# Layer 1 of a graph network: scatter sums over 64 nodes instead of 128, two 64-column matmuls of 193 columns instead of one of 385

## What is computed

```
w   = silu(edge_scalars @ Wfc1/4) @ (Wfc2/8)             # 192 weights per edge
e0, e1 = f0[src], f1[src]                                # 64 scalars, 32 vectors of the source node
mid0 = w0 * e0 * y0            (64)                      # y: 4 numbers per edge
mid1 = w3 * dot(e1, y1) / sqrt(3)   (32)
mid2 = w1 * e0 * y1            (3 x 64)
mid3 = w2 * e1 * y0            (3 x 32)
n    = segment_sum([mid0, mid1, mid2, mid3], dst) / max(count(dst), 1)
out  = x + sc + (n_scalars @ Wa) * (n @ Wl2)             # per node
```

## Time and profile before

| | |
|---|---|
| time, median of 3 runs | 8661.65 us (8655.53 to 8667.87) |
| span of the profiled execution | 8679.9 us |
| PE busy in the span | 7627.6 us (88%) |
| DVE busy | 7274.4 us (84%) |
| POOL busy | 6016.9 us (69%) |
| ACT busy | 3252.4 us (37%) |
| layer 1, first to last gather issue | 6421 to 8600 us of the span |
| last stage (`node2`) | from 8614.9 us |

### The profile page before, as it was taken

How to read it: one execution, slowest core, us unless ns; L and a number is a source line. 1 busy time by engine, 2 the same in 40 slices (tenths; PEclk the granted TensorE clock), 3 DMA queues, 4 the chain that set the end, 5 groups by cost and what they waited for, 6 DMA issues and landing times. The chain is left out here.

```text
span 8679.9 us, 218293 instructions
## 1 busy us (share of the span) xinstructions
PE 7627.6 (88%) x60373; PEld 5771.5 (66%) x60374; DVE 7274.4 (84%) x17597; ACT 3252.4 (37%) x8375; POOL 6016.9 (69%) x5890
## 2 busy tenths in 40 slices
PE   2599999999999999999999999887968888888888
PEld 1487777877877787877787778776644444444445
DVE  4699999999999999999999999775368888888886
ACT  1244444444444444444444444332222222222223
POOL 0477777777777777777777777651037777777774
PEclk9799999999999999999999999987569999999999
DMA  4344444444444444444444444321012222222222
GB/s 53 78 101 99 102 100 101 102 100 101 101 102 101 101 101 99 102 100 100 100 101 102 101 102 100 77 75 29 11 37 67 67 67 67 67 67 67 67 67 61
DMA packets 616622, 725.52 MB, mean 84 GB/s; under 512 B 284132, under 2 KB 390884, under 8 KB 616573
## 3 DMA queue, kind: packets, MB, share of 16 engines
q0 software_dynamic: 225408, 385.00, 20.4%
q1 hardware_dynamic: 391165, 339.92, 15.3%
HBM read 708.40 MB, written 16.06 MB: 83 GB/s over the span
## 5 line engine op out<-in xcount | busy, mean ns | idle before, releaser
L778 PE MATMUL bank_pair<-w_msg,blocks 128*128 128x160 f32 (+2 forms) x15640 | 2078.7, 288 | 126.8 <-DVE blocks L1030 98.2
L720 POOL DMA_INDIRECT got_src<-src_tab,idx x1564 | 1661.5, 1062 | 659.4 <-POOL idx L714 358.5
L778 PEld LDWEIGHTS bank_pair<-w_msg,blocks 128*128 128x128 f32 x15640 | 1972.7, 192 | 218.5 <-DVE blocks L1030 218.5
L1504 POOL DMA_INDIRECT gotf<-f_tab,idx x1568 | 1702.3, 1086 | 514.2 <-issue 477.4
L720 POOL DMA_INDIRECT got_dst<-dst_tab,idx x1564 | 1486.3, 950 | 528.7 <-issue 503.7
L802 PEld LDWEIGHTS bank_pair<-weights_t,product 128*128 128x128 f32 x12896 | 1498.7, 195 | 309.9 <-issue 295.6
L802 PE MATMUL bank_pair<-weights_t,product 128*128 128x128 f32 x12896 | 1575.5, 281 | 9.5 <-ACT weights_t L932 8.2
L1545 PE MATMUL bank_pair<-val,to_node 128*128 128x385 f32 x3136 | 1247.6, 545 | 5.0 <-DVE val L1659 5.0
L1600 ACT ACTIVATE val<-pre,y_edge 128x160 f32<-128x160 f32 x1568 | 542.8, 417 | 1534.0 <-DVE pre L1640 1531.4
L1545 PEld LDWEIGHTS bank_pair<-val,to_node 128*128 128x128 f32 x3136 | 621.6, 208 | 536.8 <-issue 270.1
L767 PE MATMUL bank_pair<-edge,w_edge 64*128 64x512 f32 x3128 | 884.8, 642 | 9.5 <-DVE blocks L1030 9.5
(11 more groups left out here) (268 smaller groups left out, 11950.3 us busy)
## 6 DMA issues: line engine op xcount, KB each, us to landing
rbf<-in_rbf SPq DMA_DIRECT2D x391, 256.0 KB
dst_bc<-in_dst_rows SPq DMA_DIRECT2D x391, 256.0 KB
y<-in_y SPq DMA_DIRECT2D x391, 128.0 KB
y<-in_y SPq DMA_DIRECT2D x391, 96.0 KB
gotf<-f_tab,idx POOLq DMA_INDIRECT x1568, 2.7
got_src<-src_tab,idx POOLq DMA_INDIRECT x1564
got_dst<-dst_tab,idx POOLq DMA_INDIRECT x1564
rbf<-in_rbf SPq DMA_DIRECT2D x392, 32.0 KB, 1.7
```

Of the source, the lines that this page charges most:

```text
L720: pool.indirect_dma_start(out=buf[slot][:, t, :], out_offset=None, in_=table[:, :], in_offset=bass.IndirectOffsetOnAxis(ap=idx[slot][:, c: ...
L778: return nc.tensor.matmul(to, blocks[rows, k, P * t:P * t + P], w_msg[rows, c0:c1], start=start, stop=stop)
L1504: pool.indirect_dma_start(out=got[k][:, t, :], out_offset=None, in_=f_tab[:, :], in_offset=bass.IndirectOffsetOnAxis(ap=idx[k][:, t:t + 1] ...
```

## The change

A pair now sums over a window of 64 nodes (`WIN`), and `marks` counts blocks of 64. The mask has 64 columns for each tile in place of 128. The 385 columns become two halves of 192, each with a column of ones after it (193): half 0 holds the 160 columns that ACT writes and the 32 of L1659, half 1 the 192 of L1652. For each tile two matmuls, with the same mask as stationary operand, write half 0 to PSUM partitions 0 to 63 and half 1 to partitions 64 to 127, on the two 64-column halves of the array. `win` and `total` are then 128 partitions by 193 columns: partition p and p + 64 hold the two halves of the same node. `total` has 99 blocks of 193 columns in place of 50 of 385. In the last stage a tile of 128 nodes takes two blocks: four transposes of 128 columns, and for each half of the nodes four matmuls with a 64-column stationary operand. A small copy on DVE brings the counts to the right partitions, and the set-up has three more small DVE instructions.

```diff
-SUM1 = SUM + 1
+HALF = SUM // 2
+HALF1 = HALF + 1
+WIN = 64
+NB1 = NODES_PAD // WIN
...
-    w_last = sb("w_last", [P, 3, QW - 1])
+    w_last = sb("w_last", [P, 4, QW - 1])
...
-    total = sb("total", [P, NT + 1, SUM1])
+    total = sb("total", [P, NB1 + 1, HALF1])
...
-                    pool.memset(total[:, 0:12, :], 0.0)
+                    pool.memset(total[:, 0:24, :], 0.0)
...
+                    chain.step(dve.tensor_copy(col_i[:], iota_col[:]))
+                    chain.step(dve.tensor_scalar(col_i[:], col_i[:], WIN - 1, None, ALU.bitwise_and))
+                    chain.step(dve.tensor_copy(col[:], col_i[:]))
...
-                    chain.step(dve.tensor_scalar(slot0[:], slot0[:], float(P), None, ALU.is_lt))
+                    chain.step(dve.tensor_scalar(slot0[:], slot0[:], float(WIN), None, ALU.is_lt))
...
-                    chain.step(dve.tensor_scalar(span_i[:], span_i[:], 7, None, ALU.logical_shift_right))
+                    chain.step(dve.tensor_scalar(span_i[:], span_i[:], 6, None, ALU.logical_shift_right))
...
-        to_node = [tmp(f"to_node1{i}", [P, TILES, P]) for i in range(2)]
+        to_node = [tmp(f"to_node1{i}", [P, TILES, WIN]) for i in range(2)]
...
-        win = [psum[3][:, 512 * i:512 * i + SUM1] for i in range(2)]
+        win = [psum[3][:, 512 * i:512 * i + HALF1] for i in range(2)]
...
+                def add_tile(half, nodes, k, t, start, stop):
+                    for side in range(2):
+                        last = nc.tensor.matmul(win[half][WIN * side:WIN * side + WIN, :], nodes,
+                                                val[k][:, t, HALF1 * side:HALF1 * side + HALF1], start=start, stop=stop)
+                    return last
+
...
-                        last = nc.tensor.matmul(win[k // 2], to_node[k % 2][:, t, :], val[k][:, t, :],
-                                                start=k % 2 == 0 and t == 0, stop=k % 2 == 1 and t == TILES - 1)
+                        last = add_tile(k // 2, to_node[k % 2][:, t, :], k, t, k % 2 == 0 and t == 0, k % 2 == 1 and t == TILES - 1)
...
-                    for j, n in enumerate(rows_of):
-                        last = nc.tensor.transpose(pT[t % 2][0:n, j, :], total[:, t, P * j:P * j + n], ident[:])
+                    for j in range(4):
+                        first = WIN * (j % 2)
+                        last = nc.tensor.transpose(pT[t % 2][:, j, :], total[:, 2 * t + j // 2, first:first + P], ident[:])
...
-                    for j, n in enumerate(rows_of):
-                        last = nc.tensor.matmul(pQ[t % 2], turned[t % 2][0:n, j, :], w_last[0:n, j, :], start=j == 0, stop=j == 2)
+                    for k in range(4):
+                        cols = slice(WIN * (k // 2), WIN * (k // 2) + WIN)
+                        for part in range(2):
+                            last = nc.tensor.matmul(pQ[t % 2][WIN * part:WIN * part + WIN, :], turned[t % 2][:, 2 * part + k % 2, cols],
+                                                    w_last[:, k, :], start=k == 0, stop=k == 3)
...
-                    nc.scalar.activation(turned[t % 2][:], pT[t % 2][:, 0:3, :], ACT.Copy).then_inc(S["turned_copied"], 1)
+                    nc.scalar.activation(turned[t % 2][:], pT[t % 2], ACT.Copy).then_inc(S["turned_copied"], 1)
...
+                    for part in range(2):
+                        rows = slice(WIN * part, WIN * part + WIN)
+                        last = dve.tensor_copy(den[rows, :], total[rows, 2 * c * CH + part:2 * (c + 1) * CH:2, HALF])
+                    chain.step(last)
```

More of the change, by code:

```diff
@@ L233, in _ @@
                 for k, frm, c in last_pieces(A):
-                    put(w_last[k % P:k % P + frm.shape[0], k // P, c:c + frm.shape[1]], frm)
+                    half, place = k // HALF, k % HALF
+                    upper = place >= P
+                    place -= WIN if upper else 0
+                    put(w_last[place:place + frm.shape[0], 2 * half + upper, c:c + frm.shape[1]], frm)
                 sp.wait_ge(s_ext, 2)
@@ L479, in last_pieces @@
         for part in range(2):
-            out.append((D + CS * x + 32 * part, v[32 * part:32 * part + 32, :], c))
-    k = D + 3 * CS
+            out.append((HALF + CS * x + 32 * part, v[32 * part:32 * part + 32, :], c))
+    k = D
     out += [(k, s[64:96, :], 0), (k, a[64:96, :], CS)]
@@ L1354, in tmp @@
             return sx.enter_context(nc.sbuf_tensor(name, shape, dt))
-        val = [tmp(f"val{i}", [P, TILES, SUM1]) for i in range(4)]
+        val = [tmp(f"val{i}", [P, TILES, 2 * HALF1]) for i in range(4)]
         slot0 = tmp("slot0", [P, NG_PAD * TILES])
@@ L1362, in layer1 @@
         more_from = tmp("more_from", [1, PAIRS + 1], I32)
-        steps = tmp("steps", [P, 64])
+        steps = tmp("steps", [P, 128])
+        col = tmp("col1", [P, 1])
         with ExitStack() as tx:
@@ L1555, in body @@
                             for t in range(2 * TILES):
-                                last = nc.tensor.matmul(win[half], to_more[:, t, :], val[2 * half + t // TILES][:, t % TILES, :],
-                                                        start=t == 0, stop=t == 2 * TILES - 1)
+                                last = add_tile(half, to_more[:, t, :], 2 * half + t // TILES, t % TILES, t == 0, t == 2 * TILES - 1)
                             last.then_inc(s["more_sum"], 1)
@@ L1670, in merge @@
                     q, half = i * 2 + k // 2, k // 2
-                    row, count = nc.s_assert_within(mark & 63, 0, NT - 1), mark >> 6
+                    row, count = nc.s_assert_within(mark & 127, 0, NB1 - 1), mark >> 7
                     dve.wait_ge(s["window_sum"], q * 2 + 2)
@@ L1684, in more @@
                     done = w * 8
[L1685 removed]
+                    nth = nc.s_assert_within(w - first + 1, 0, 127)
                     def settled(instruction, n):
@@ L1728, in node2 @@
             "turned", "turned_copied", "mapped", "mapped_copied", "ch", "res", "out0", "out1")}
-        turned = [tmp(f"turned{i}", [P, 3, P]) for i in range(2)]
+        turned = [tmp(f"turned{i}", [P, 4, P]) for i in range(2)]
         q = [tmp(f"q{i}", [P, CH, QW - 1]) for i in range(2)]
```

64 lines of the change are left out of this document (33 added, 31 removed).

## The result

The changed kernel takes 8714.6 us, median of 4 runs (8710.43 to 8716.64), against 8660.49 us (4 runs, 8655.53 to 8667.87) for the kernel before, measured beside it: 1.0063 times, 95% interval 1.0049 to 1.0077. It is slower by 54 us, where 73 were forecast. The profiled execution has a span of 8708.6 us, 28.7 more than the one of before. That difference is smaller than the medians' because the profiled execution of before was slow for its kernel: layer 0, which the edit doesn't touch, took 20.3 us more in it than in the one after. From the start of layer 1's set-up (the fill of `total`) to the end, the two executions took 2300.1 and 2349.2 us, 49.1 apart.

The account below looks back on a forecast made before the run. Layer 1's loop was taken as bound by a ring of DVE and gathers, the last stage by PE. Set-up 1, loop 0, further windows 30 and last stage 42 gave +73 us: 8735 us, range 8695 to 8795.

Parts of the forecast that it names:

- The ring: Layer 1's loop: L1636 to end of L1652 3.06 us, held gather's end 0.81, landing 1.72; together 5.59 us.
- one gather of 1.5 us per group: Sign listed for the loop: each group would show a gather of 1.5 us.
- The loop: Layer 1's loop: DVE's 1.16 us saved per pair turns into waiting for rows; 0 taken, bounds -20 and +12 us.
- The window sum on PE: Layer 1's loop: eight slots of two side-by-side passes take 1.7 us against 2.6 before, worth 0.
- The further windows: Layer 1's loop: five pairs spanning 64 nodes or more run `more`; the last four cost +30 us, bounds 21 and 52.
- M: Price of one `more` on DVE in layer 1's loop: 10.9 us, bounds 8.7 and 16.5.
- pair 181 is hidden: Layer 1's loop: this pair's `more` costs nothing, POOL running about 11 us ahead and DVE regaining its lag later.
- The last stage: PE's 49 tiles behind the loop: 2.01 us each, +0.86 per tile, +42 us in all; bounds +19 and +78.
- slots without overhead: Rival: paired passes cost one duration, slots 0.134 and 0.161 us; last stage +19 to 24, M 10.1; 8711 us, chance 0.12.
- the two changes of width: Last stage: PE changing between 128 and 64 columns loses 0.05 us each time, 0.1 per tile.
- The adds: DVE in layer 1's loop: an add of 193 columns takes 0.31 us, 0.31 less each, two per pair.
- the set-up: Ahead of layer 1's loop: three more chained DVE instructions and a few POOL fills, +1.3 us, all on the path.

Follow-up runs that it names:

- e6b_before_late: Kernel before with DVE's product L1652 moved later, behind L1657, same work, run again in the third batch: 8656.20 us, 1.0020 of the kernel before.
- a0_after_again: The changed kernel itself, unaltered, measured once more in the third batch: 8689.57 us, 1.0050 of the kernel before.
- e1_no_more: Changed kernel with the number of further windows set to 0 for all pairs, their edges left out: 8665.82 us, 1.0022 of the kernel before.

## Why the prediction came out as it did

**The direction and the bound were right.** The loop's pace is that of the gathers, and PE and DVE got 38 us per 500 us of relief that turned into waiting. The ring's signs are there as listed: period 5.54 us, DVE waiting for rows in 325 of 343 groups, starts of the two halves together. One sign was too simple: not one gather of 1.5 us per group, but in 206 of 342 groups two held ones, mostly for 0.15 to 0.4 us. And the ring is less than a fixed path: what set the pace in every run is four gathers and their pauses, and the landing and L1652 only decide where the gathers start; `e6b_before_late` missed by taking it for more.

**The loop: 0 taken, -6.9 us up to group 365.** It lies inside the bounds of -20 and +12. The gathers are 5 ns shorter in the mean, and 4 x 0.005 x 365 is 7 us. `a0_after_again` has 2014.4 us for groups 0 to 363, where the two executions of before and after have 2019.0 and 2012.1, so a part of it is the spread between executions. In the first batch three kernels with this same loop took 1997.4 to 1998.2 us for it, so the batch moves it by more than the 6.9.

**The window sum on PE.** 1.53 us at full clock for 16 passes, against 1.7 forecast and 2.86 (eight passes of twice the width) before, and worth nothing in the loop. The granted clock fell from 0.94 to 0.75 with PE busy for 376 instead of 414 us of 500, and that cost nothing either: at the low level the sum takes 2.84 us, and DVE waits 11.2 us for it in all.

PE in the loop of the kernel after, at the full level and, a group later, at the low one; `L1536` and `L1537`, on the two halves of the array, start together.

```profile
7111.40 0.42 PE L1536 MATMUL bank_pair<-rbf,w_fc 16*64 16x256 f32 x1
7111.41 0.42 PE L1537 MATMUL bank_pair<-rbf,w_fc 16*64 16x256 f32 x1
...
7111.98 1.53 PE L1553 MATMUL bank_pair<-val,to_node 128*64 128x193 f32 x16
...
7117.77 2.84 PE L1553 MATMUL bank_pair<-val,to_node 128*64 128x193 f32 x16
```

**The further windows: +30 taken, +29.7 for the last four.** The number of loops, their places and the price held: M comes out at some 10.4 us (the three intervals with a `more` between groups 385 and 391 have a mean of 15.45 us, less the 5.0 of a group with a merge), where 10.9 was put. Inside it terms were off against each other, and that part is luck: the entry takes 0.9 to 1.2 us for 1.5, the eight small steps 1.8 to 2.2 for 2.6, and DVE waits 5.1 to 5.8 us for PE's part, where 4.7 and 0.25 for handing over were put. Wrong was "pair 181 is hidden": it isn't hidden but pays back more than it costs, 10.2 against 17.3 us, because for fourteen groups behind it the gathers are held less. The prediction counted only that DVE regains its lag up to the ring's pace, not that it gets past it.

**The last stage: +42 taken, +33 measured.** This is the term that was mis-sized, and it explains 9 of the 24 us between the sums. The slot was taken from the 16-row pair at 0.184 us where 128 rows give 0.138 (the rival "slots without overhead" had this right), 0.37 us too much in a tile; the two changes of width were put at 0.1 where they cost 0.30, 0.2 too little. Together 1.84 for 2.01 us, by 49.

**The adds** cost 0.42 us for 193 columns where the line through two sizes gave 0.31, but they start 0.33 us apart, and it is hidden in the loop.

Of the 24 us between 73 and 49, 9 are the last stage, 7 the loop up to group 365, 7 pair 181's pay-back and 1 the set-up. The measured 8714.6 lies nearer to the 8711 of the rival "slots without overhead" than to 8735. That is in part luck: the rival was right on the slots, but it put the changes of width at 0 to 0.05 us each, where they cost 0.15, and had neither of the 7 us.

## What to carry to other kernels

When two engines have slack and the loop doesn't get faster, look at what the third one's instructions collide with: here the order of DVE's instructions, with no work added or taken away, was worth 0.5% before the change and over 1% after it, more than the whole change cost. Price a change that narrows tiles at its edges as well: the passes overlap for free, each change of width costs 0.15 us here, where PE is the bound. And a rare branch was free in the middle of a loop with buffers ahead, and four at its end, with nothing behind them to catch up in, cost 33 us of their 42.

## What the runs showed of the hardware

- A gather that starts while a DVE instruction with both inputs in SBUF runs (L1627, L1644 and L1652 before, L1644, L1661 and L1669 after) ends 0.81 to 0.83 us after that instruction does, or after its own 0.945 us if that is later: it can take up to 1.75 us (`e6b_before_late`). The first 0.03 us of the DVE instruction are an exception: in the kernel before, 6500 to 8400 us, 68 gathers start up to 0.034 us behind it and none is held; all 546 that start later than that, with 0.2 us or more of the instruction left, are. The Trainium skill ("SBUF — State Buffer", Who interferes with whom) has a DVE instruction with two SBUF inputs contend with a GpSimd instruction that reads SBUF; the traces agree for an indirect gather.
- The pause of 0.305 us between gathers is the same in all kernels. What makes it was not tried.
- Batches differ: in one the kernel before took 9947.62 us, in the others 8637.64 to 8660.49. The slow batch and the third carry the same chip number, so whether the chip makes the difference is open. The loop in the first batch had gathers of 1.071 us in `e1_no_more` where `a0_after_again` has 1.083 in the third, with the same loop. The gather alone and the pause are the same in both; the product costs the gathers 77 us there and 122 here, `along` 96 and 67. Why they fall so is open.
